# A recommender tower on one core: layer 2 takes layer 1's blocks in the order they are formed, and each block is signalled and copied on its own

## The reference, cut to what matters

```python
# 2048 samples, 40 embedding tables, 64 numbers to a row, float32 throughout
e = stack([tbl_f[ids[:, f]] for f in range(40)], axis=1)        # 2048 x 40 x 64
z[b, p] = (e[b, i_p] @ L0_rec_W[p]) . e[b, j_p]                 # 780 pairs i < j
h = concatenate([z, dense_ctx], axis=1)                         # 780 + 16 = 796
h = maximum(h @ W_top1 + b_top1, 0)                             # layer 1: 796 -> 512
h = maximum(h @ W_top2 + b_top2, 0)                             # layer 2: 512 -> 256
y = h @ W_top3                                                  # layer 3: 256 -> 1
```

## Time and profile before

| | |
|---|---|
| median of 3 runs (lowest, highest) | 1158.18 us (1156.47, 1160.94) |
| the profiled execution's own time | 1160.57 us |
| its span, first to last instruction | 1158.8 us |
| PE matmul busy | 1105.2 us, 95% of the span |
| DVE busy | 947.9 us, 82% |
| ACT busy | 859.5 us, 74% |
| POOL busy | 744.8 us, 64% |
| TensorE's mean granted clock | 0.994 of full speed |

### The profile page before, as it was taken

The page is one execution under the profiler, slowest core; times in us unless marked ns, Lnnn a source line. Parts: engine busy times, 40 slices in busy tenths (PEclk is TensorE's granted clock), DMA queues, the critical chain, the costliest instruction groups (busy, mean ns, idle before and its releaser), DMA issues.

```text
span 1158.8 us, 52361 instructions
## 1 busy us (share of the span) xinstructions
PE 1105.2 (95%) x21232; PEld 506.7 (44%) x21232; DVE 947.9 (82%) x830; ACT 859.5 (74%) x6607; POOL 744.8 (64%) x898
## 2 busy tenths in 40 slices
PE   2699989999999999999999999999999999999998
PEld 1356757665643333333363333333354333333333
DVE  0699878999859689999976689999984968999960
ACT  0677857999958569999965457898982845799971
POOL 7776777777756555778777567788777756522310
PEclk9999999999999999999999999999999999999999
DMA  6344444444423332232322232222222323211000
GB/s 187 83 121 131 125 121 121 130 139 130 103 52 87 86 88 72 76 86 76 77 63 78 71 93 76 76 78 77 77 68 49 94 73 93 70 58 58 19 3 18
DMA packets 60594, 98.02 MB, mean 85 GB/s; under 512 B 17072, under 2 KB 17088, under 8 KB 60352
## 3 DMA queue, kind: packets, MB, share of 16 engines
q1 hardware_dynamic: 35568, 64.57, 18.1%
q0 software_dynamic: 20480, 21.01, 9.3%
q10 hardware_dynamic: 4304, 9.09, 2.4%
HBM read 94.60 MB, written 0.01 MB: 82 GB/s over the span
## 4 chain that ended last, share of the span: by engine, by line
PE 76%; ACT 9%; POOL 5%; issue 5%; DVE 4%; DMA 1%; DVEq 0%; POOLq 0%
PE u L1038 30%; PE u L1024 18%; PE zacc L1052 15%; ACT row_prod L838 8%; PE u L1084 7%; PE u L996 3%; POOL gathered L734 3%; DVE prod L952 2%; PE u L1096 2%; POOL first_fields L734 1%; DVE row_prod L921 1%; POOL row_prod_p L755 1%; DMA gathered<-tbl,index 1%; PE u L1090 1%; PE u L1070 0%
## 5 line engine op out<-in xcount | busy, mean ns | idle before, releaser
L838 ACT ACTIVATE row_prod<-row_prod 128x64 f32<-128x64 f32 x3248 | 776.5, 242 | 65.9 <-DVE row_prod L921 65.7
L952 DVE TENSOR_TENSOR prod<-u,emb 128x1024 f32<-128x1024 f32 x496 | 588.8, 1217 | 102.0 <-PE u L1038 100.4
L734 POOL DMA_INDIRECT gathered<-tbl,index x512 | 484.7, 947 | 221.9 <-issue 121.5
L838 ACT ACTIVATION_READ_ACCUMULATOR row_prod<-row_prod 128x1 f32 x3248 | 613.1, 189 | 0.0
L1038 PE MATMUL u<-emb,weights 64*32 64x512 f32 (+1 forms) x9760 | 523.1, 507 | 3.5 <-DVE prod L952 2.1
L1024 PE MATMUL u<-row_weights,emb 64*32 64x512 f32 (+5 forms) x5632 | 337.7, 522 | 7.1 <-ACT emb L799 2.3
L1038 PEld LDWEIGHTS u<-emb,weights 64*32 64x32 f32 x9760 | 200.9, 107 | 235.7 <-issue 114.4
L921 DVE TENSOR_TENSOR row_prod<-u,first_fields 128x1024 f32<-128x1024 f32 x203 | 246.9, 1216 | 62.1 <-PE u L1024 61.8
L1052 PE MATMUL zacc<-prod,band 64*32 64x512 f32 (+1 forms) x4960 | 277.1, 504 | 0.7 <-DVE prod L952 0.5
L755 POOL TENSOR_TENSOR row_prod_p<-row_prod_p 128x512 f32<-128x512 f32 (+4 forms) x210 | 128.8, 614 | 90.8 <-DVE row_prod_p L921 77.1
L1024 PEld LDWEIGHTS u<-row_weights,emb 64*32 64x32 f32 x5632 | 118.4, 109 | 147.4 <-issue 56.7
(11 more groups left out here) (29 smaller groups left out, 151.9 us busy)
## 6 DMA issues: line engine op xcount, KB each, us to landing
weights<-w_pairs SPq DMA_DIRECT2D x155, 256.0 KB
row_weights<-w_rows SPq DMA_DIRECT2D x90, 256.0 KB
gathered<-tbl,index POOLq DMA_INDIRECT x512
w12s<-w_top ACTq DMA_DIRECT2D x8, 832.0 KB
first_fields<-tbl,index POOLq DMA_INDIRECT x128
w12s<-w_top ACTq DMA_DIRECT2D x4, 512.0 KB
index<-ids SPq DMA_DIRECT2D x1, 280.0 KB, 11.8
row_sums<-dense ACTq DMA_DIRECT2D x4, 32.0 KB
```

The costliest lines, as they stand in the source:

```text
L734: pool.indirect_dma_start(out=to, out_offset=None, in_=tables[2 * t + e], in_offset=bass.IndirectOffsetOnAxis(ap=index[:, col:col + 1].bit ...
L838: last = nc.scalar.activation(x, x, ACT.Copy, accum_out=row_sums[:, c % 2, s, q:q + 1])
L952: nc.vector.tensor_tensor(result, products, x, ALU.mult).then_inc(prod_ready, 1)
```

## The change

PE gets a second signal, `top_half`. In group 1 (layer 1, blocks 2 and 3) it is raised when block m = 0 is complete, and in group 2 (layer 2) likewise; for that the 64-row matmuls of group 1 are moved from the end of the group to its beginning. Group 0 keeps its order and its one signal. ACT waits for each half on its own (in group 0 for `top_ready` both times) and signals `top_copied` behind every copy, so that this semaphore now counts seven copies in a chunk instead of four groups. Layer 2's eight matmuls take the blocks of layer 1 in the order 0, 0, 1, 1, 2, 2, 3, 3 (m alternating), with three waits: for blocks 0 and 1, for block 2 and for block 3. Layer 3 waits before each of layer 2's blocks on its own.

```diff
@@ -386,6 +386,10 @@
 
 FULL = ZG - 1
 W12_BLOCKS = 2 * FULL + 1
+
+
+TOP_COPIES = M1 + M2 + 1
+LAYER1_COPIES = range(1, M1 + 1)
 
 
 def make_needs():
@@ -671,6 +675,7 @@
         sums_done = sem("sums_done")
         z_copied = sem("z_copied")
         top_ready = sem("top_ready")
+        top_half = sem("top_half")
         top_copied = sem("top_copied")
         out_stored = sem("out_stored")
         block = ctx.enter_context(nc.Block())
@@ -841,7 +846,6 @@
             def copy_top(c, group, o):
                 layer, first = TOPS[group]
                 acc = u[:, BUFFER[o], :, :]
-                act.wait_ge(top_ready, c * TOP_GROUPS + group + 1)
                 if group == 0:
                     act.wait_ge(small_loaded, 3 * 16)
                     if c:
@@ -849,17 +853,22 @@
                         act.wait_ge(out_stored, c * 16)
                 if layer < 3:
                     for m in (0, 1):
+                        if m == 0 and group:
+
+                            act.wait_ge(top_half, c * (TOP_GROUPS - 2) + group)
+                        else:
+                            act.wait_ge(top_ready, c * TOP_GROUPS + group + 1)
                         to, bias = (h1, b1s) if layer == 1 else (h2, b2s)
-                        ins = nc.scalar.activation(to[:, first + m, :], acc[:, m, :], ACT.Relu,
-                                                   bias=bias[:, first + m:first + m + 1])
+                        nc.scalar.activation(to[:, first + m, :], acc[:, m, :], ACT.Relu,
+                                             bias=bias[:, first + m:first + m + 1]).then_inc(top_copied, 1)
                 else:
-                    ins = nc.scalar.activation(ysb, acc[:, 0, 0:P], ACT.Copy)
-                ins.then_inc(top_copied, 1)
+                    act.wait_ge(top_ready, c * TOP_GROUPS + group + 1)
+                    nc.scalar.activation(ysb, acc[:, 0, 0:P], ACT.Copy).then_inc(top_copied, 1)
                 next_load = c * (TOP_GROUPS - 1) + group + 2
                 if layer < 3 and next_load < CHUNKS * (TOP_GROUPS - 1):
                     load_w12(next_load)
                 if layer == 3:
-                    act.wait_ge(top_copied, (c + 1) * TOP_GROUPS)
+                    act.wait_ge(top_copied, (c + 1) * TOP_COPIES)
                     act.dma_start(y[c, :, :], ysb[0:P:TILE, :]).then_inc(out_stored, 16)
 
             for o in ORDER:
@@ -981,7 +990,7 @@
                 elif last[0] == "turn":
                     pe.wait_ge(z_copied, Z_COPY[last[1], ROW_BLOCK + 2 * last[2], 0])
                 else:
-                    pe.wait_ge(top_copied, last[1] * TOP_GROUPS + last[2] + 1)
+                    pe.wait_ge(top_copied, last[1] * TOP_COPIES + min(2 * last[2] + 2, TOP_COPIES))
 
             def transpose_step(c, i, q, b):
                 for h in (0, 1):
@@ -1076,32 +1085,50 @@
                 if layer < 3:
                     pe.wait_ge(w12_loaded[x % 2], (x // 2 + 1) * 16)
                 if layer == 1:
+                    def remainder(start):
+                        for m in (0, 1):
+                            half = slice(m * DIM, (m + 1) * DIM)
+                            last = nc.tensor.matmul(u[:, b, m, :], w12s[half, x % 2, 2 * FULL, :], z_blocks(c, FULL)[half, 0, :],
+                                                    start=start, stop=not start)
+                        return last
+
+
+                    if first:
+                        remainder(True)
                     for m in (0, 1):
                         for q in range(FULL):
                             if first + m == 0:
                                 pe.wait_ge(z_copied, Z_COPY[(c, ROW_BLOCK, 0) if q >= ROW_BLOCK else
                                                             (c, q // 2, len(parts(c)) - 1)])
-                            nc.tensor.matmul(u[:, b, m, :], w12s[:, x % 2, m * FULL + q, :], z_blocks(c, q)[:, 0, :],
-                                             start=(q == 0), stop=False)
+                            last = nc.tensor.matmul(u[:, b, m, :], w12s[:, x % 2, m * FULL + q, :], z_blocks(c, q)[:, 0, :],
+                                                    start=(first == 0 and q == 0), stop=(first > 0 and q == FULL - 1))
+                        if first and m == 0:
+                            last.then_inc(top_half, 1)
                     if first == 0:
                         pe.wait_ge(z_copied, Z_COPY[c, ROW_BLOCK + 2, 0])
-                    for m in (0, 1):
-                        half = slice(m * DIM, (m + 1) * DIM)
-                        last = nc.tensor.matmul(u[:, b, m, :], w12s[half, x % 2, 2 * FULL, :], z_blocks(c, FULL)[half, 0, :],
-                                                start=False, stop=True)
+                        last = remainder(False)
                 elif layer == 2:
 
-                    pe.wait_ge(top_copied, c * TOP_GROUPS + group)
-                    for m, q in itertools.product((0, 1), range(M1)):
+
+                    for m, q in ((0, 0), (1, 0), (0, 1), (1, 1), (1, 2), (0, 2), (0, 3), (1, 3)):
+                        if (m, q) == (0, 0):
+                            pe.wait_ge(top_copied, c * TOP_COPIES + LAYER1_COPIES[1])
+                        elif (m, q) == (1, 2):
+                            pe.wait_ge(top_copied, c * TOP_COPIES + LAYER1_COPIES[2])
+                        elif (m, q) == (0, 3):
+                            pe.wait_ge(top_copied, c * TOP_COPIES + LAYER1_COPIES[3])
                         last = nc.tensor.matmul(u[:, b, m, :], w12s[:, x % 2, m * M1 + q, :], h1[:, q, :],
                                                 start=(q == 0), stop=(q == M1 - 1))
+                        if (m, q) == (0, M1 - 1):
+                            last.then_inc(top_half, 1)
                 else:
                     pe.wait_ge(small_loaded, 3 * 16)
-                    pe.wait_ge(top_copied, c * TOP_GROUPS + group)
-
-                    for q, g in itertools.product(range(M2), range(SUB)):
-                        last = nc.tensor.matmul(u[g * TILE:(g + 1) * TILE, b, 0, 0:P], w3s[:, q, :],
-                                                h2[:, q, g * P:(g + 1) * P], start=(q == 0), stop=(q == M2 - 1))
+
+                    for q in range(M2):
+                        pe.wait_ge(top_copied, c * TOP_COPIES + M1 + q + 1)
+                        for g in range(SUB):
+                            last = nc.tensor.matmul(u[g * TILE:(g + 1) * TILE, b, 0, 0:P], w3s[:, q, :],
+                                                    h2[:, q, g * P:(g + 1) * P], start=(q == 0), stop=(q == M2 - 1))
                 last.then_inc(top_ready, 1)
 
             pe.wait_ge(ident_made, 2)
```

## The result

The changed kernel takes 1156.25 us (median of 19 runs, 1153.59 to 1157.9), the kernel before 1158.18 (19 runs, 1155.19 to 1160.99). The prediction was 1156.3. Measured twice more beside the kernel before, the ratio was 0.9979 [0.9968, 0.9989] and, on a chip on which everything took longer, 0.9983 [0.996, 1.0005], which alone would show no difference.

A forecast was written before the change was run, and what follows sets the result against it. PE was taken to bound the long middle, and PE-ACT handovers the end. Savings of 2.45 us at the end less 0.60 lost in the middle gave 1.85, so 1156.3 us against 1158.18, range 1154.0 to 1158.9.

The forecast's parts named there:

- Short matmuls first, at the end: Chunk 3, layer 1: group 1's 64-row matmuls follow group 0's in the same array shape; 0.22 us saved.
- Layer 2 without its wait: Chunk 3, between layers 1 and 2: all three waits are met when PE reaches them; 1.43 us saved.
- One copy before layer 3 instead of two: Chunk 3: layer 2's first half is copied under its second, leaving one copy; 0.59 us saved.
- Half of layer 3 ahead: Chunk 3: layer 3's first half runs before the second copy lands; 0.21 us saved.
- The middle: Chunks 0 to 2, group 1: one more change of array shape, 0.20 us, in three groups; 0.6 us lost.
- Waits and signals at zero: PE's added waits and signals, 20 in all: taken to cost zero, at worst 4.0 us.
- B: Rival, middle: ACT's earlier half copies count, six groups giving 3.5 us, so 1152.8 us; chance 4%.
- C: Rival, groups 1 to 3 of all chunks: added waits and shape changes outweigh the gain, up to 1160.3 us; chance 9%.
- D: Rival, end: early signal brings nothing, two copies still follow layer 1; 1.05 us saved, 1157.1 us; chance 5%.
- A: Rival, layer-1 groups: clock or a gather falls otherwise, one slow stretch of 1.7 us; 1154.6 or 1158.0; chance 15%.

The follow-up runs named there:

- e2: Changed kernel with group 1's 64-row matmuls left last in every chunk, all else as changed; 1156.38 us, ratio 0.9973 to the kernel before.
- one-wait kernel: Changed kernel with layer 2 in its new order but waiting at its start for all four blocks of layer 1; 1157.98 us, ratio 0.9992 to the kernel before.
- e9: Changed kernel with layer 2's two blocks copied together and layer 3 waiting for both; 1157.23 us, ratio 0.9986 to the kernel before.
- e5: Changed kernel with 60 more long-met waits before full matmuls of groups 1 and 2 in chunks 0 to 2; ratio 0.9987 to the kernel before.
- e6: Changed kernel with 78 more signals that nobody waits for, on matmuls of layers 1 and 2 in chunks 0 to 2; ratio 0.9988 to the kernel before.

## Why the prediction was right

The forecast was 1156.3 and the time is 1156.25; its mechanism held at each step. Three terms were off in size, two too small and one too large.

- *Short matmuls first, at the end: 0.22 us.* The layer-1 pieces took 1.92 + 10.50 = 12.42 in place of 12.64 us, 0.22 as forecast. The kernel that never moves them (e2) takes 0.41 more at the end: about 0.2 of it in layer 1 and 0.2 in layer 2, whose 7.08 us hold a change of shape that the kernel before had under its copies.
- *Layer 2 without its wait: 1.43 us.* The ACT piece and both small gaps are gone. **Undersized by 0.24:** I let layer 2 keep its 7.12 us, but that length belonged to a PE that starts anew after idling. In a stream it takes 6.88 here and 6.87 in the middle, a row that I had before me. The one-wait kernel brought the 7.12 back together with the copy.
- *One copy before layer 3 instead of two: 0.59 us.* From layer 2's end to layer 3's it was 0.02 + 1.27 + 0.14 + 0.68; now it is 0.02 + 0.70 + 0.04 + 0.47. **Undersized by 0.08:** the gap after the copy fell from 0.14 to 0.04 us, which I hadn't foreseen, while the copy takes 0.70 where I had 0.68. In the pair-copy kernel (e9) the gap is 0.14 again.
- *Half of layer 3 ahead: 0.21 us.* 0.68 to 0.47, as forecast.
- *The middle: 0.6 us lost.* **Oversized by 0.11:** 0.20 in two groups and 0.09 in the third, as I had taken one group's row for all three. Where the drain at a change of tiling mode, as the Trainium skill calls it ("TensorEngine Tiling (Array Packing)", Key Properties), could be seen by itself, it cost the 0.20 read off before.
- *Waits and signals at zero.* Shown for waits and signals that are met or unneeded, in full-width matmuls of 512 samples, on one chip (e5, e6).

The rows thus give 2.77 - 0.49 = 2.28 us where the prediction summed 1.85; the measured ratios 0.9982 and 0.9979 are 2.1 and 2.4 us. So 1156.25 agrees with 1156.3 more closely than the sum deserved. The terms missed by 0.24 + 0.08 + 0.11 = 0.43 us, all on the same side, and the noise of the medians covered it: that is luck.

Of the rivals, B and C were tried and fell. D (the early signal brings nothing) turned out half right: layer 1's early signal does bring nothing, though it comes early, and layer 2's brings the 0.88 us of copy and layer 3. A wasn't tried, but the granted clock goes with the spread of the runs. In the 68 runs of the kernel before that stood beside the experiments on the two like chips, the 23 with a mean granted clock of 0.991 or less have a median of 1160.73 us, the 21 with 0.996 or more 1158.26. This 2.5 us is as much as the whole change, and a reason why one pair of profiles (4.2 us apart) must not be read as its effect. That the clock is the cause and not a companion of longer idle times wasn't tried.

Which parts are worth keeping follows from the same rows: separate waits in layer 2 (1.11 us if put back to one), layer 2's half signal with separate waits in layer 3 (0.88), and the moved matmuls in the last chunk alone (0.41 there, and 0.49 saved in the middle by leaving them).

## What to carry to other kernels

At the end of a kernel, where stages can no longer be mixed with other work, split a handover by blocks: wait for each input block where it is first read, and signal an output block on its own where that shortens what follows. Check in the trace how much work stands before the first late block; if it is longer than the copies, as the 3.4 us here, neither the order of the matmuls nor an earlier signal matters for that handover. An edit to shared code that helps at the end also runs in the middle, where only the bound engine's time counts: here moving two small matmuls cost as much in three places in the middle (0.49 us by the rows) as it gave at the end (0.41). When a change is worth a fifth of a per cent, sum it from the pieces of the chain and let the timed runs only confirm the sign.

## What was not expected of the hardware

**A PE that resumes.** Layer 2's sixteen matmul records take 6.87 or 6.88 us in a stream and 7.12 us after the engine has waited for a copy; the 0.24 us comes on top of the wait itself. (In the second chunk they take 7.00 or 7.01 us although PE doesn't stop; why is open.) The gap between a copy's end and PE's next start is 0.14 us after two copies back to back and 0.04 after a single one before layer 3, yet 0.14 after a single one before layer 2 in the one-wait kernel. So it isn't the number of copies that decides. Nor is it the time for which PE stood: in the kernel before, PE idled 2.3 us for gathered rows, and the gap at its end, at 883.09 us, was 0.04. What decides stays open.

**A chip on which PE stands still among small matmuls.** On one chip the same kernels took some 490 us more. The timeline of PE there, in the changed kernel (last column: idle time before):

```profile
1002.25 1.01 PE L1061 MATMUL zacc<-prod,band 64*32 64x512 f32 x2 [0.42 <-issue]
1003.67 1.01 PE L1061 MATMUL zacc<-prod,band 64*32 64x512 f32 x1 [0.41 <-issue]
```

and the same kind of step in the kernel before on the first chip:

```profile
1004.77 1.07 PE L1052 MATMUL zacc<-prod,band 64*32 64x512 f32 x16
```

Where sixteen records of small matmuls make one piece of 1.07 us on the one, one or two stand between gaps of 0.4 us on the other, and nothing that the profile knows ends the gaps ("issue"). The gaps are the smaller part of the loss: of the 491.7 us by which the span is longer than that of the changed kernel on the first chip, PE idles 122.6 more (172.1 against 49.5), and for 369.1 more it counts as busy (1474.2 against 1105.1), with fewer matmuls side by side. The mean granted clock is lower too, 0.959 against 0.994, and 0.79 in the 6 us around these rows; whether that is a cause or follows from the gaps, the trace doesn't say. The full-width matmuls of layer 1, of which far fewer are issued in a microsecond (24 records in 10.30 us, against 16 in 0.86), took 10.30 and 10.50 us on both. That speaks for the supply of instructions to PE rather than to its array; it wasn't tried, and what differed in that chip is open.
